# Moving half of a normalisation from VectorE to GpSimd at the head of its step, in the first pass of a two-pass expert FFN

## The chip, the core and the metric

The kernel runs on one core of one Trainium2 chip. The metric is the device time of one execution in microseconds (us), as a median of several runs.

## The reference

The input is 16384 tokens of 128 floats (256 x 64 positions). A first layer adds a gated pair-mixing block to it. The second layer, which the change concerns, is a mixture of eight experts, each token going to two of them:

```python
def _L0_ffn_ref(x, Wr, br, ln_g, ln_b, W1, b1, W2, b2):      # D = 128, E = 8 experts, H = 512
    probs = softmax(xt @ Wr + br)
    top_p, top_idx = top_k(probs, 2)
    weights = top_p / top_p.sum(axis=-1, keepdims=True)
    xn = (xt - mu) * rsqrt(var + 1e-5)
    xe = xn[None] * ln_g[:, None, :] + ln_b[:, None, :]
    h = gelu(einsum('end,edh->enh', xe, W1) + b1[:, None, :])
    y = einsum('enh,ehd->end', h, W2) + b2[:, None, :]
    out = (weights[:, :, None] * take_along_axis(y by token, top_idx)).sum(axis=1)
t = t + out
```

## The kernel before

Up to about 465 us of the profiled execution the kernel does the first layer, the choice of experts, and the scatter of each token's row (128 floats of data and a few of its own: scale `RS`, shift `SH`, weights, addresses) into a table in DRAM, sorted by expert. Then come two passes over tiles of 256 rows, 70 tiles each. A tile has two halves (`HALVES`, `b` = 0 and 1) of 128 rows. The first pass takes every token at its first expert, the second at its second. In the first pass a tile's rows are read from `row_dram`, normalised on the chip (the row's own `RS` and `SH`), and stored to `row2_dram` with the result added and with the normalised row beside it, so that the second pass has nothing to normalise.

Every engine runs its own queue, written out by `two_lists`: at step k it does each of its stages for the tile k minus that stage's lag, in the order of the list. Six slots (`RING`) hold the tiles; the body of the loop is six steps. In the first pass step k is:

- SyncE (`load_tile`): waits until both stores of tile k-6 have landed (`o_stored`, L339) and issues the load of a tile (L340). It runs ahead as far as the slots let it.
- VectorE: `norm(k)`, two operations, one for each half (L986); `xT_low(k-1)` (L991); `h_low(k-2)` for the first part (L996), `mix(k-3)` of half 0 (L1002), `h_low(k-2)` for the second part, `mix(k-3)` of half 1.
- TensorE: `xT(k-1)`, two transposes (L1158); `up(k-2)` in two parts (L1182 to L1184), with a reading of the experts' numbers between them in every sixth step (`next_experts`); `down(k-3)` (L1193 to L1204).
- ScalarE: `xT_high(k-1)` (L598), then `gelus(k-2)` in two parts (L605, L608).
- GpSimd: `store_tile(k-3)`, an indirect DMA for each half (L428), each after a wait for the `mix` of that half (`y_done`).

The names in the trace leave out numbers: `B` holds the tile's slots (`Rw`), `AB` the hidden values, `PPb` the split weights, `ps` PSUM.

Of the kernel before, what the change touches and what calls it, by code (L numbers as in the profile page):

```python
# [7 lines left out]
ALU = mybir.AluOpType  # L8
# [9 lines left out]
NE, D, H = 8, 128, 512  # L18
# [4 lines left out]
HALVES = 2  # L23
# [4 lines left out]
RING = 6  # L28
# [12 lines left out]
ROW = D + 8  # L41
ROW2 = ROW + D
R1, RS, SH, WLO, WHI, TOK, POS = range(D, D + 7)
# [19 lines left out]
def two_lists(eng, stages, depth, before=None, always=None):  # L63

    longest = max(lag for lag, _ in stages)
    for second, low, high in ((0, 0, CUT), (1, CUT, TILES)):

        def step(n, u):
            if before:
                before(n, u, low)  # L70
            for lag, stage in stages:
                if not isinstance(n, int) or low <= n - lag < high or stage is always and n + 1 < high + longest:
                    stage(n - lag, (u - lag) % RING, second)

        def single(n0, n1):
            for n in range(n0, n1):
                step(n, n % RING)

        first, last = -(-(low + longest + depth) // RING), high // RING
        single(low, first * RING)  # L80
        with eng.Fori(first, last) as t:
            for u in range(RING):
                step(t * RING + u, u)
        single(last * RING, high + longest)


def build(nc, x, pp, cp, z_mask, ln_w, ln_b, lnc_w, lnc_b, gate_w, gate_b, lin_w, lin_b, eg_w, eg_b,
          as_w, as_b, Wr, br, ffn_g, ffn_b, W1, b1, W2, b2, out, g_dram, row_dram, row2_dram):
    with ExitStack() as ctx:
# [3 lines left out]
        def sem(name):  # L93
            return ctx.enter_context(nc.semaphore(name))
# [88 lines left out]
        class Choice:  # L183
# [28 lines left out]
        Rw = Bf[:, 0:RING * HALVES * ROW2].rearrange("p (s b r) -> p s b r", s=RING, b=HALVES)  # L212
# [10 lines left out]
            "tail w_given rank_psum keep_set tail_done "  # L223
            "table Q_done tbl_psum cnt_done tbl_done pads_out pad_set "
            "gbM_step f_step ft_setup gb_kept am_done w1_sum w1_high w2_high b3f_dma "
            "store_next fill_done b23_zero xn_done xT_psum xT_hi xT_lo".split())}
        s = type("S", (), S)
        x_loaded = [sem(f"x_loaded{u}") for u in range(XRING)]
        pp_in = [[sem(f"pp_in{h}_{u}") for u in range(2)] for h in range(IC)]
# [8 lines left out]
        r_loaded = [sem(f"r_loaded{u}") for u in range(RING)]  # L238
# [10 lines left out]
        def _(sp):  # L249
# [64 lines left out]
            for table, blank, g0 in ((row_dram, pad, 0), (row2_dram, pad2, NE)):  # L314
                for q in range(0, NE, 4):
                    _, counts = nc.values_load_multi_w_load_instructions(nti[0:1, 1, g0 + q:g0 + q + 4], [mybir.EngineType.SP],
                                                                         min_val=0, max_val=N)
                    for k in range(4):
                        sp.dma_start(pair(table[bass.ds(counts[k] + (q + k) * CAP, TR), :]), blank).then_inc(s.pads_out, 16)
# [6 lines left out]
            for b, (_, j0, j1) in enumerate(BATCHES):  # L326
                sp.wait_ge(scattered[b], 16 * (j1 - j0))
# [17 lines left out]
        def _(pool):  # L345
# [84 lines left out]
                                            Rw[:, u, b, 0:D] if second else Rw[:, u, b, :], None,  # L430
                                            bounds_check=last_token if second else last_row, oob_is_err=False).then_inc(o_stored[u], 16)

            two_lists(pool, [(3, store_tile)], 1)
            for u in range(RING):
                pool.wait_ge(o_stored[u], 16 * HALVES * len(range(u, TILES, RING)))

# [1 line left out]
        def _(act):  # L438
# [65 lines left out]
            def weights(b):  # L504

                _, j0, j1 = BATCHES[b]
                act.wait_ge(s.tail, TAIL * b + 15)
                for at, scale in ((WLO, 1.0), (WHI, -1.0)):
                    a = act.activation(rows[:, j0:j1, at:at + 1].rearrange("p j o -> p (j o)"), choices[j1 - j0].m12[:, DL, :],
                                       ACT.Sigmoid, scale=scale)  # L510
                a.then_inc(s.w_given, 1)
# [101 lines left out]
        def _(dve):  # L613
# [339 lines left out]
            for e in range(NE):  # L953
                i = dve.scalar_tensor_tensor(W2h[:, e, 1, :, :], W2s[:, e, :, :], SCALE, W2h[:, e, 0, :, :], ALU.mult, ALU.subtract)
# [20 lines left out]
            for v, table in enumerate((first_row, experts[:, EFRONT:EFRONT + TILES])):  # L975
                i = dve.tensor_copy(table.rearrange("p (l t) -> p l t", l=LISTS),
                                    ps[6 + v][0:1, 0:LISTS * P].rearrange("p (l t) -> p l t", l=LISTS)[:, :, 0:CUT])
            i.then_inc(s.tbl_done, 1)

            def norm(n, u, second):  # L980

                if second:
                    return
                dve.wait_ge(r_loaded[u], (n // RING) * 16 + 16)
                for b in range(HALVES):
                    i = dve.tensor_scalar(Rw[:, u, b, ROW:ROW2], Rw[:, u, b, 0:D], Rw[:, u, b, RS:RS + 1], Rw[:, u, b, SH:SH + 1], ALU.mult, ALU.add)  # L986
                i.then_inc(s.xn_done, 1)

            def xT_low(n, u, second):
                dve.wait_ge(s.xT_hi, n + 1)  # L990
# [7 lines left out]
            def mix(n, u, second, b):  # L998
# [4 lines left out]
                                         ALU.mult, ALU.add).then_inc(y_done[b], 1)  # L1003

            two_lists(dve, [(0, norm), (1, xT_low), (2, lambda n, u, second: h_low(n, u, 0)), (3, lambda n, u, second: mix(n, u, second, 0)),
                            (2, lambda n, u, second: h_low(n, u, 1)), (3, lambda n, u, second: mix(n, u, second, 1))], 2)

        @block.tensor
        def _(pe):
# [54 lines left out]
            for h in range(IC):  # L1064
# [7 lines left out]
                for m in range(BANKS):  # L1072
# [7 lines left out]
                    for a in range(2):  # L1080
# [6 lines left out]
                        if m == 0 and a == 0:  # L1087
                            pe.wait_ge(s.abT_copied, h * 8 + 8)
                            pe.wait_ge(s.cp_done, 2)
                        i = pe.matmul(o.rearrange("p (x j) -> p x j", x=4)[:, 0::3, :], ABT[:, c // 2, :],  # L1090
                                      CPz[:, c:c + 2, :], start=False, stop=(a == 1))
# [53 lines left out]
            for k in range(2 * NQ):  # L1145
                i = pe.matmul(ps[6 + k // NQ][0:1, k % NQ * P:(k % NQ + 1) * P], Q[:, k:k + 1], ident[:, :], start=True, stop=True)
# [5 lines left out]
            def xT(n, u, second):  # L1152
                if second:
                    pe.wait_ge(r_loaded[u], (n // RING) * 16 + 16)
                else:
                    pe.wait_ge(s.xn_done, n + 1)
                for b in range(HALVES):
                    i = pe.transpose(ps[u % 2][:, b * P:(b + 1) * P], Rw[:, u, b, ROW:ROW2], ident[:, :])  # L1158
                i.then_inc(s.xT_psum, 1)
# [48 lines left out]
            def next_experts(n, u, second):  # L1208
                if u == RING - 1:
                    load_experts(n + 1)  # L1210

            two_lists(pe, [(1, xT), (2, lambda n, u, second: up(n, u, 0)), (0, next_experts), (2, lambda n, u, second: up(n, u, 1)),
                           (3, lambda n, u, second: down(n, u))], 2, before=begin, always=next_experts)

# [22 lines left out]
```

## Time and profile before

| | |
|---|---|
| three timed runs | 972.84, 979.42, 980.21 us (median 979.42) |
| the profiled execution | 973.23 us, its span 971.3 us |
| busy in the span | PE 737.7, VectorE 613.6, ScalarE 583.6, GpSimd 490.6 us |
| mean granted TensorE clock | 0.912 |

The span runs from the first to the last instruction; some 1.9 us of the profiled execution lie outside it. All times in the trace count from the span's start. The first pass fills the stretch from about 465 to 722 us, the second from there to the end. A busy share says what an engine did over the stretch, not whether others waited for it.

### The profile page before, as it was taken

What the parts mean: (1) busy time and instruction counts of PE and PEld (TensorE: products, weight loads), DVE (VectorE), ACT (ScalarE), POOL (GpSimd) and SP (SyncE); (2) the same over time, 40 slices, a digit from 0 to 9 for tenths busy, and PEclk for the clock granted to TensorE, in tenths of its full rate; (3) what the DMA queues carried; (4) which work ended last, traced back from release to release, by engine and by line L of the source; (5) the groups of instructions that cost most, each with busy time, mean ns of one, the idle gap of its engine ahead of it and who ended that gap; (6) DMA issues with size and microseconds to landing.
All of it is one profiled execution on the core that took longest, in us unless ns stands there. A gap on an engine that the chain in (4) does not pass through costs nothing. (4 is left out here: it accounts for less than half of the span.)

```text
span 971.3 us, 24094 instructions
## 1 busy us (share of the span) xinstructions
PE 737.7 (76%) x7308; PEld 644.9 (66%) x7309; DVE 613.6 (63%) x1866; ACT 583.6 (60%) x1162; POOL 490.6 (51%) x539
## 2 busy tenths in 40 slices
PE   1877899467696475622699999899859999999995
PEld 1655689255596365511588877778748888889884
DVE  6556510647843579876478777778746666667663
ACT  2667643579443366232477777767637777777773
POOL 4556500000177713777255555655644566666664
PEclk9989999679799588766799999999989999999998
DMA  7978510758113573415233333333323334434341
GB/s 217 236 226 260 153 55 10 228 147 261 58 57 120 181 231 108 163 55 200 70 114 114 113 119 113 117 106 114 111 65 110 116 113 120 125 115 127 117 130 30
DMA packets 127286, 126.86 MB, mean 131 GB/s; under 512 B 22472, under 2 KB 95455, under 8 KB 127107
## 3 DMA queue, kind: packets, MB, share of 16 engines
q1 hardware_dynamic: 92914, 82.73, 29.1%
q0 software_dynamic: 15296, 34.64, 10.1%
q10 hardware_dynamic: 19024, 8.86, 3.3%
q8 instruction: 26, 0.43, 0.2%
q14 instruction: 26, 0.21, 0.1%
HBM read 79.48 MB, written 49.09 MB: 132 GB/s over the span
## 5 line engine op out<-in xcount | busy, mean ns | idle before, releaser
L996 DVE TENSOR_TENSOR AB<-AB 128x512 f16<-128x512 f32 x280 | 192.2, 686 | 48.0 <-ACT AB L608 47.7
L399 POOL DMA_INDIRECT row_dram<-rows,idx x128 | 128.5, 1004 | 164.5 <-DVE rows L791 126.5
L605 ACT ACTIVATE AB<-ps 128x512 f16<-128x512 f32 x280 | 168.2, 601 | 56.2 <-PE ps L1184 55.9
L428 POOL DMA_INDIRECT row_dram<-B x140 | 143.4, 1025 | 115.4 <-DVE B L1002 79.3
L428 POOL DMA_INDIRECT out<-B x140 | 148.8, 1063 | 92.8 <-DVE B L1002 47.3
L1201 PE MATMUL ps<-PPb,AB 128*128 x1120 | 185.5, 219 | 0.0
L1202 PE MATMUL ps<-PPb,AB 128*128 x1120 | 185.4, 219 | 0.0
L1182 PE MATMUL ps<-B,PPb 128*128 128x256 f16 x560 | 154.7, 276 | 20.4 <-issue 10.2
L608 ACT ACTIVATE AB<-ps 128x512 f32<-128x512 f32 x280 | 168.9, 603 | 0.0
L1183 PE MATMUL ps<-B,PPb 128*128 128x256 f16 x560 | 154.2, 275 | 0.0
L1204 PE MATMUL ps<-PPb,AB 128*128 x1120 | 154.2, 219 | 0.0
L1184 PE MATMUL ps<-B,PPb 128*128 128x256 f16 x560 | 154.1, 275 | 0.0
L1002 DVE SCALAR_TENSOR_TENSOR B<-ps,B 128x128 f32<-128x128 f32 x280 | 97.2, 348 | 43.3 <-PE ps L1204 42.2
L598 ACT ACTIVATE B<-ps 128x256 f16<-128x256 f32 x140 | 53.7, 384 | 108.2 <-PE ps L1158 108.0
L1202 PEld LDWEIGHTS ps<-PPb,AB 128*128 128x128 f16 x1120 | 109.6, 98 | 0.0
L1201 PEld LDWEIGHTS ps<-PPb,AB 128*128 128x128 f16 x1120 | 108.6, 98 | 0.5
L1158 PE MATMUL ps<-ident,B 128*128 128x128 f32 x280 | 58.2, 290 | 46.4 <-DVE B L986 32.4
L1204 PEld LDWEIGHTS ps<-PPb,AB 128*128 128x128 f16 x1120 | 86.0, 98 | 0.0
L986 DVE TENSOR_SCALAR B<-B 128x128 f32<-128x128 f32 x140 | 44.0, 368 | 57.9 <-DMA B<-row_dram 57.2
L1182 PEld LDWEIGHTS ps<-B,PPb 128*128 x560 | 55.1, 98 | 36.3 <-issue 29.8
L1085 PE MATMUL ps<-AB,PPb 128*128 128x128 f32 x512 | 67.8, 276 | 1.2 <-DVE AB L698 1.2
L1045 PE MATMUL ps<-Wz,work 128*128 128x256 f32 x256 | 66.7, 408 | 0.7 <-ACT work L475 0.7
(214 smaller groups left out, 1350.2 us busy)
## 6 DMA issues: line engine op xcount, KB each, us to landing
B<-row_dram SPq DMA_DIRECT2D x70, 264.0 KB
B<-row_dram SPq DMA_DIRECT2D x70, 136.0 KB
rows<-in_x SPq DMA_DIRECT2D x32, 256.0 KB, 5.0
rows<-in_L_conv_protein_pair SPq DMA_DIRECT2D x16, 512.0 KB, 4.6
g_dram<-work ACTq DMA_DIRECT2D x32, 256.0 KB, 2.8
work<-g_dram SPq DMA_DIRECT2D x32, 256.0 KB, 3.9
ABT<-in_x SPq DMA_DIRECT2D x32, 256.0 KB, 4.2
ABT<-in_L_conv_protein_pair SPq DMA_DIRECT2D x16, 512.0 KB, 4.1
```

What stands on the lines that cost most here:

```text
L399: pool.indirect_dma_start(row_dram, bass.IndirectOffsetOnAxis(ap=idx[:, j:j + 1], axis=0), rows[:, j, :], None).then_inc(scattered[b], 16)
L428: pool.indirect_dma_start(out_rows if second else row2_dram, bass.IndirectOffsetOnAxis(ap=Rw[:, u, b, at:at + 1].bitcast(u32), axis=0), Rw ...
L605: act.activation(Hp[:, hs, 0, :], ps[HB[hs]][:, :], ACT.Gelu, scale=1.0 / SCALE)
L608: act.activation(Hf[:, q, :], ps[HB[hs]][:, :], ACT.Gelu, scale=1.0 / SCALE).then_inc(h_full[q], 1)
L996: dve.tensor_tensor(Hp[:, hs, 1, :], Hf[:, q, :], Hp[:, hs, 0, :], ALU.subtract).then_inc(h_parts[q], 1)
L1002: dve.scalar_tensor_tensor(Rw[:, u, b, 0:D], ps[4 + b][:, 0:D], Rw[:, u, b, w:w + 1], Rw[:, u, b, 0:D], ALU.mult, ALU.add).then_inc(y_done ...
L1182: pe.matmul(o, w(0), xTp[:, u % 2, 0, :], start=True, stop=False)
L1183: pe.matmul(o, w(0), xTp[:, u % 2, 1, :], start=False, stop=False)
L1184: i = pe.matmul(o, w(1), xTp[:, u % 2, 0, :], start=False, stop=True)
L1201: pe.matmul(ps[4 + b][:, 0:D], hk(0, b), w(0), start=False, stop=False)
L1202: pe.matmul(ps[4 + b][:, 0:D], hk(1, b), w(0), start=False, stop=False)
L1204: i = pe.matmul(ps[4 + b][:, 0:D], hk(0, b), w(1), start=False, stop=(k == HC - 1))
```

## The change

In the first pass `norm` on VectorE keeps half 0 only. GpSimd gets a new first stage of lag 0, `norm_second(k)`, which normalises half 1 of tile k, ahead of the stores of tile k-3 in its queue. TensorE's `xT` waits for both. In the second pass the new stage returns at once, as `norm` does.

```diff
@@ gpsimd
-            two_lists(pool, [(3, store_tile)], 1)
+            def norm_second(n, u, second):
+                if second:
+                    return
+                pool.wait_ge(r_loaded[u], (n // RING) * 16 + 16)
+                pool.sem_inc(s.store_next, 1)
+                pool.tensor_scalar(Rw[:, u, 1, ROW:ROW2], Rw[:, u, 1, 0:D], Rw[:, u, 1, RS:RS + 1], Rw[:, u, 1, SH:SH + 1],
+                                   ALU.mult, ALU.add).then_inc(s.xn_done2, 1)
+
+            two_lists(pool, [(0, norm_second), (3, store_tile)], 1)
@@ vector
                 dve.wait_ge(r_loaded[u], (n // RING) * 16 + 16)
-                for b in range(HALVES):
-                    i = dve.tensor_scalar(Rw[:, u, b, ROW:ROW2], Rw[:, u, b, 0:D], Rw[:, u, b, RS:RS + 1], Rw[:, u, b, SH:SH + 1], ALU.mult, ALU.add)
-                i.then_inc(s.xn_done, 1)
+                dve.tensor_scalar(Rw[:, u, 0, ROW:ROW2], Rw[:, u, 0, 0:D], Rw[:, u, 0, RS:RS + 1], Rw[:, u, 0, SH:SH + 1],
+                                  ALU.mult, ALU.add).then_inc(s.xn_done, 1)
@@ tensor
                     pe.wait_ge(s.xn_done, n + 1)
+                    pe.wait_ge(s.xn_done2, n + 1)
```

## Rows read from the trace of the kernel before

**Rows 1.** The busy time of each engine in one stretch (from the windows view).

```profile
core 0: us, PE busy (x) PEld busy (x) DVE busy (x) ACT busy (x) POOL busy (x), PEclk, DMA share, GB/s
600.00:620.00 20.00, 18.03 (x229) 15.98 (x227) 14.39 (x38) 14.06 (x29) 11.84 (x12) 1.00 0.37 116
```

**Rows 2.** Waits, 500 to 700 us: us in total, times, longest.

```profile
DVE B L986 <- DMA B<-row_dram: 35.5, 33, 3.0
...
PEld ps L1182 <- issue: 15.3, 24, 2.0
```

**Rows 3.** Waits of the queue of SyncE, 500 to 700 us.

```profile
SPq L339 <- DMA row_dram<-B: 103.7, 54, 4.2
```

**Rows 4.** Line L986: ns min/median/max, first and last start.

```profile
L986 DVE TENSOR_SCALAR B<-B x140: 331/346/609, 468.3 to 708.2; 128x128 f32<-128x128 f32 x140
```

**Rows 5.** Timeline of VectorE: start, us, operation, idle before and releaser.

```profile
573.14 0.59 DVE L986 TENSOR_SCALAR B<-B 128x128 f32<-128x128 f32 x2
...
575.00 0.35 DVE L1002 SCALAR_TENSOR_TENSOR B<-ps,B 128x128 f32<-128x128 f32 x1 [0.24 <-PE ps L1204]
...
577.81 0.68 DVE L986 TENSOR_SCALAR B<-B 128x128 f32<-128x128 f32 x2 [1.60 <-DMA B<-row_dram]
...
579.26 0.34 DVE L1002 SCALAR_TENSOR_TENSOR B<-ps,B 128x128 f32<-128x128 f32 x1
...
587.69 0.60 DVE L986 TENSOR_SCALAR B<-B 128x128 f32<-128x128 f32 x2 [1.08 <-DMA B<-row_dram]
```

**Rows 6.** Timeline of GpSimd, the same steps.

```profile
574.48 1.14 POOL L428 DMA_INDIRECT row_dram<-B  x1 [0.30 <-issue]
576.17 0.98 POOL L428 DMA_INDIRECT row_dram<-B  x1 [0.55 <-issue]
577.45 0.98 POOL L428 DMA_INDIRECT row_dram<-B  x1 [0.30 <-issue]
580.43 0.98 POOL L428 DMA_INDIRECT row_dram<-B  x1 [1.99 <-DVE B L1002]
581.72 0.98 POOL L428 DMA_INDIRECT row_dram<-B  x1 [0.30 <-issue]
```

**Rows 7.** Timeline of the queue of SyncE, one load.

```profile
584.99 0.54 SPq L340 DMA_DIRECT2D B<-row_dram  x1
```

**Rows 8.** Timeline of TensorE, the transposes of four steps.

```profile
568.83 0.43 PE L1158 MATMUL ps<-ident,B 128*128 128x128 f32 x2
...
571.86 0.39 PE L1158 MATMUL ps<-ident,B 128*128 128x128 f32 x2
...
574.85 0.39 PE L1158 MATMUL ps<-ident,B 128*128 128x128 f32 x2
...
578.54 0.44 PE L1158 MATMUL ps<-ident,B 128*128 128x128 f32 x2 [0.54 <-DVE B L986]
```

**Rows 9.** Timeline of weight loads, the first of `up`'s second part, some rounds.

```profile
503.47 0.10 PEld L1182 LDWEIGHTS ps<-B,PPb 128*128 x1 [0.76 <-issue]
...
525.43 0.10 PEld L1182 LDWEIGHTS ps<-B,PPb 128*128 x1 [1.61 <-issue]
...
609.37 0.10 PEld L1182 LDWEIGHTS ps<-B,PPb 128*128 x1 [2.00 <-issue]
...
713.54 0.10 PEld L1182 LDWEIGHTS ps<-B,PPb 128*128 x1 [0.89 <-issue]
```

**Rows 10.** Line L378, the first layer's normalisation on GpSimd.

```profile
L378 POOL TENSOR_SCALAR work<-rows x96: 441/445/552, 18.7 to 121.1; 128x128 f32<-128x128 f32 x96
```

**Rows 11.** Timeline of GpSimd: an indirect DMA and what follows it.

```profile
439.23 0.96 POOL L399 DMA_INDIRECT row_dram<-rows,idx  x1 [0.30 <-issue]
440.19 0.34 POOL L412 MEMSET work<- 128x272 f32 x1
```

**Rows 12.** Both engines at once (timelines), and line L996.

```profile
504.61 0.98 POOL L428 DMA_INDIRECT row_dram<-B  x1 [0.30 <-issue]
```

```profile
504.80 0.85 DVE L986 TENSOR_SCALAR B<-B 128x128 f32<-128x128 f32 x2 [1.49 <-DMA B<-row_dram]
```

```profile
L996 DVE TENSOR_TENSOR AB<-AB x280: 674/683/762, 473.8 to 957.7; 128x512 f16<-128x512 f32 x140
```

More of the change, by code:

```diff
@@ L225, in build @@
             "gbM_step f_step ft_setup gb_kept am_done w1_sum w1_high w2_high b3f_dma "
-            "store_next fill_done b23_zero xn_done xT_psum xT_hi xT_lo".split())}
+            "store_next fill_done b23_zero xn_done xn_done2 xT_psum xT_hi xT_lo".split())}
         s = type("S", (), S)
```

## The prediction

> **What bounds the kernel now.** I read the busy shares of a stretch of the first pass first. TensorE is busy 18.03 of 20 us, VectorE 14.39 and GpSimd 11.84 [rows 1]: at the mean step neither VectorE nor GpSimd is full, so a shift of work between them pays only where it shortens a chain. The step's mean comes from the first and last `norm`: (708.2 - 468.3) / 69 = 3.477 us [rows 4].
>
> The waits come next. VectorE's `norm` waited 33 times, 35.5 us in all, for the load of its tile [rows 2], and the load itself waited: SyncE stood 103.7 us, 54 times, at the stores of the tile that held the slot before [rows 3]. So the first pass runs in a ring through memory. Follow it in the timelines: `norm` starts at 577.81; `mix` of half 0 runs from 579.26 to 579.60; its store starts at 580.43 and the second store ends at 582.70; the load that needs the slot is issued at 584.99; the `norm` of that tile, three steps later, starts at 587.69, released by the DMA [rows 5 to 7]. That is 1.79 + 0.83 + 2.27 + 2.29 + 2.70 = 9.88 us for three steps; the mean of three steps is 10.43.
>
> The second chain to be read is the one through TensorE, which today has room. Its transposes at 571.86 open a step of TensorE, and the `mix` that ends that step starts at 575.00, released by TensorE; the stores follow at 576.17 and 577.45 and end at 578.43 [rows 5, 6, 8]. From transposes to end of stores: 6.57 us, made of 3.14 (TensorE's step), 0.35 (`mix`), 0.82 (to the start of the store) and 2.26 (two stores). One step earlier it is 575.62 - 568.83 = 6.79 [rows 6, 8]. TensorE's own step is 574.85 - 571.86 = 2.99 us.
>
> Third, TensorE has a stall of its own once in a round of six steps, ahead of the second part of `up`, where the experts' numbers are read: 0.76, then 1.61, and so on in turn, once 2.00, in a step whose transposes had begun late [rows 9]. Ten rounds lie between 503.47 and 713.54: 21.0 us each.
>
> **The change, part by part.**
>
> *VectorE loses one operation.* The pair takes 0.59 or 0.60 us and a single one 0.346 [rows 4, 5], so what goes is 0.25 us a step, 17.5 us of busy time over 70 steps. Of this only what stands in a binding chain counts. In the memory ring `norm` stands once per three steps, so the most that can come back is 0.25 x 70 / 3 = 5.8 us.
>
> *GpSimd gains one operation.* Its length is that of the same operation of the same shape in the first layer, 0.445 us [rows 10]. The nearest row for its start behind an indirect DMA is a memset that starts at 440.19, just as the DMA ends (439.23 + 0.96): no gap. Between two indirect DMAs there are 0.30 us [rows 11]. So the gap is 0 to 0.30; I take 0.05, since the 0.30 goes with the set-up of a DMA. GpSimd then needs 0.445 + 2.27 + 0.55 (the gap ahead of a tile's first store [rows 6]) + 0.05 = 3.3 us a step, against 3.48: GpSimd alone does not become the bound.
>
> *TensorE gains a wait, and here is the price.* The operation stands behind both stores of tile k-4 in GpSimd's queue, though its tile may have landed long before. Put it into today's rhythm. For the `norm` at 577.81 the stores end at 578.43, so half 1 is ready at 578.43 + 0.445 = 578.88, and with 0.05 us to the next engine (today's `norm` ends at 578.49 and the transposes start at 578.54) the transposes could start at 578.93, not 578.54 [rows 5, 6, 8]. For the `norm` at 573.14 the stores end at 575.62 and the transposes could start at 576.12, not 574.85 [rows 5, 6, 8]. So it is late by 0.4 and 1.3 us, and it is late in nearly every step. Behind the waiting transposes all of TensorE's step is queued: `up` of tile k-2 and `down` of tile k-3. On `down` waits `mix`, on `mix` the store, and behind the store stands the next normalisation but one. That closes a new ring of two steps: `norm_second(k-1)`, transposes of k-1, `down(k-3)`, `mix(k-3)`, `store_tile(k-3)`, `norm_second(k+1)`.
>
> Its length, low: 0.445 + 0.05 + 6.57 + 0 = 7.07 us; high: 0.445 + 0.05 + 6.79 + 0.30 = 7.59; taken, with the mean of the two samples: 0.445 + 0.05 + 6.68 + 0.05 = 7.23, or 3.61 a step. The stall for the experts falls on the same one of the two interleaved rings each time, since six is even, so it adds to every third turn of that ring, and the other can't run ahead of it. It is 1.2 (mean of 0.8 and 1.6) to 2.0; I take 1.6, because TensorE will now stand at its transposes in each step, as it had before the 2.00. A round of six steps is then 3 x 7.23 + 1.6 = 23.3 us against 21.0; low 3 x 7.07 + 1.2 = 22.4, high 3 x 7.59 + 2.0 = 24.8. The ring acts from about the fifth tile on, 65 steps or 10.8 rounds: (23.3 - 21.0) x 10.8 = +25 us, low +15, high +41.
>
> *Where the memory ring's waits go.* The load leaves the slot's stores behind by 2.29 + 2.70 = 5.0 us, the new `norm_second` comes some 7 us (two steps) after those stores: the tile has landed by then, and VectorE's 35.5 us of waiting for loads should almost vanish. The gain of 0.25 us on VectorE goes with them: it ends up as idle time. What is late next is TensorE, at its transposes.
>
> *The two engines side by side.* While GpSimd prepared a store at 504.61, VectorE's pair of normalisations took 0.85 us instead of 0.60 [rows 5, 12]: the two do get in each other's way, by some 0.25 us. The same could strike the new operation, against `h_low`, which comes twice in VectorE's step. No row shows a GpSimd operation that reads its memory beside `h_low`; the bounds are 0 and one whole `h_low`, 0.68 us [rows 12]. I take 0, since in the new ring the operation starts as `mix` starts, after the first `h_low` and before the second.
>
> The Trainium skill speaks against the change here ("SBUF — State Buffer", Who interferes with whom): VectorE and GpSimd share one pair of ports under an exclusive lock, and a VectorE instruction with two inputs in SBUF, as `h_low` has, excludes a GpSimd instruction that reads SBUF for its whole length. The stretched pair agrees with it for the other kind of VectorE instruction. By the rule taken at its worst the new operation would wait behind an `h_low` in every turn of the ring, which is the second rival below.
>
> Removed and added waits of VectorE and the increments of semaphores I put at nothing; the second pass keeps its instructions but for GpSimd's empty stage, and moves as a whole.
>
> **The sum.** 973.23 (this execution) + 25 = 998. This execution is one of the low ones: the timed runs go from 972.84 to 980.21 with a median of 979.42, and on the median the sum is 1004. I forecast the middle, 1001.
>
> **The rivals.**
>
> 1. *The stall is swallowed.* If TensorE's sequencer reads the experts' numbers while it stands at the transposes, the round is 3 x 7.07 to 3 x 7.3, 21.2 to 21.9 us, +2 to +10 us: 975 to 990. For it: the stall halves in every second round. Against it: it was longest where TensorE had just stood at the transposes.
> 2. *The port decides.* Each turn of the new ring gets 0.68 us more behind an `h_low`: 3 x 0.68 x 10.8 = +22 on top of 25: 1020 to 1027. For it: the 0.85 us pair. Against it: the place of the operation in the ring.
> 3. *Not slower: the memory ring stays the bound, and VectorE's part of it is shorter.* -5.8 us at most: 967 to 974. It decides if the operation ends before TensorE is at its transposes, that is, if GpSimd's stores end at least 0.5 us (0.445 + 0.05) before them. Today they end 0.1 us before at 578.54 and 0.8 us after at 574.85, so it would take another rhythm. For it: GpSimd is only 59% busy [rows 1].
> 4. *The change does not matter*, because the operations run as said but TensorE's step stretches into slack that I haven't seen: within 5 us of before, 973 to 985.
>
> **How the numbers follow.** Forecast 0.60 (988 to 1020, from 973.2 + 15 to 979.4 + 41), the swallowed stall 0.17, the port 0.10, the shorter memory ring 0.07, no matter 0.06. Leaving out the last two and the lower part of the first rival gives 984; the top reaches into the port's case, 1023. One per cent, 9.8 us, is about what a measurement of this kernel can tell from no change: under 969.6 is the lower half of rival 3, 0.04; within it are the rest of 3, rival 4 and half of rival 1, 0.17; slower 0.79.
>
> **What would show it.** In the profile after: TensorE's transposes (L1158's successor) wait for GpSimd in nearly every step, some 0.5 us each, and that group leads the idle time of TensorE in the first pass; the waits for loads fall from 35.5 us to a few; SyncE waits longer for stores only because steps are longer; first to last `norm` is about 240 + 25 = 265 us; the GpSimd operation starts as the second store ends and takes 0.43 to 0.45 us; `h_low` keeps its 683 ns. The prediction is wrong if the transposes go on without a wait, if GpSimd's queue has the operation ahead of the stores' wait in time as well as in order, or if the second pass changes its length.

## The result and the profile after

The changed kernel takes 1028.28 us (median of four, 1024.18 to 1031.86) against 979.82 us (median of four): a ratio of 1.0507, 95% interval 1.0435 to 1.0578. That is 48 us slower, where 1001 us (984 to 1023) was forecast. The profiled execution took 1031.23 us, its span 1029.5.

Three views of the profile after say where the time went. First the windows view, the waits and SyncE's waits (500 to 700 us), for the stretches of [rows 1 to 3]. L1167 is now the transposes, L439 GpSimd's normalisation, L994 VectorE's, L1004 `h_low`, L1010 `mix`.

```profile
600.00:620.00 20.00, 15.97 (x203) 14.23 (x201) 12.98 (x30) 12.22 (x26) 14.12 (x15) 1.00 0.29 93
```

```profile
PEld ps L1167 <- issue: 39.4, 39, 1.6
PE ps L1167 <- POOL B L439: 33.7, 38, 1.5
...
PEld ps L1191 <- issue: 11.9, 8, 1.9
...
DVE B L994 <- DMA B<-row_dram: 6.8, 17, 1.7
```

```profile
SPq L339 <- DMA row_dram<-B: 121.0, 46, 5.5
```

VectorE's wait for loads, 35.5 us before, is down to 6.8, and TensorE stands at its transposes for GpSimd instead, 33.7 us in 38 waits, about 0.9 us each, in some 47 steps. SyncE stands longer at the stores, 121.0 us against 103.7, but it runs ahead, and no engine waits much for its loads. The memory ring has let go and the ring through the stores has taken over.

The lines of the two normalisations, to be set against [rows 4] and [rows 10] (min/median/max in ns, first and last start):

```profile
L439 POOL TENSOR_SCALAR B<-B x70: 447/662/1027, 471.2 to 764.7; 128x128 f32<-128x128 f32 x70
```

```profile
L994 DVE TENSOR_SCALAR B<-B x70: 328/345/391, 471.0 to 763.1; 128x128 f32<-128x128 f32 x70
```

From the first to the last `norm` there are 292.1 us, 4.23 a step, against 239.9 and 3.48: the first pass holds 52 us of the difference of the spans, 58.2; the rest lies ahead of the first `norm` (2.7) and behind the last (3.3). And GpSimd's operation takes 0.66 us at the median, where 0.445 was forecast.

One turn of each of the two interleaved rings, in the timelines of GpSimd, VectorE and TensorE:

```profile
597.39 0.65 POOL L439 TENSOR_SCALAR B<-B 128x128 f32<-128x128 f32 x1
...
600.54 0.88 POOL L439 TENSOR_SCALAR B<-B 128x128 f32<-128x128 f32 x1
602.52 1.02 POOL L428 DMA_INDIRECT row_dram<-B  x1 [1.10 <-DVE B L1010]
603.84 1.50 POOL L428 DMA_INDIRECT row_dram<-B  x1 [0.30 <-issue]
605.35 0.66 POOL L439 TENSOR_SCALAR B<-B 128x128 f32<-128x128 f32 x1
606.18 1.02 POOL L428 DMA_INDIRECT row_dram<-B  x1 [0.17 <-DVE B L1010]
607.51 0.99 POOL L428 DMA_INDIRECT row_dram<-B  x1 [0.30 <-issue]
608.52 0.87 POOL L439 TENSOR_SCALAR B<-B 128x128 f32<-128x128 f32 x1
```

```profile
600.41 0.69 DVE L1004 TENSOR_TENSOR AB<-AB 128x512 f16<-128x512 f32 x1 [0.94 <-ACT AB L617]
601.35 0.35 DVE L1010 SCALAR_TENSOR_TENSOR B<-ps,B 128x128 f32<-128x128 f32 x1 [0.24 <-PE ps L1213]
...
603.79 0.69 DVE L1004 TENSOR_TENSOR AB<-AB 128x512 f16<-128x512 f32 x1 [0.59 <-ACT AB L617]
604.72 0.35 DVE L1010 SCALAR_TENSOR_TENSOR B<-ps,B 128x128 f32<-128x128 f32 x1 [0.24 <-PE ps L1213]
604.99 0.71 DVE L1004 TENSOR_TENSOR AB<-AB 128x512 f16<-128x512 f32 x1
```

```profile
601.57 0.41 PE L1167 MATMUL ps<-ident,B 128*128 128x128 f32 x2 [0.20 <-POOL B L439]
...
606.16 0.41 PE L1167 MATMUL ps<-ident,B 128*128 128x128 f32 x2 [1.42 <-POOL B L439]
```

Normalisation 600.54 to 601.42, transposes 601.57, `mix` 604.72 to 605.07, store 606.18, end of the second store 608.50, next normalisation but one 608.52: 0.88 + 0.15 + 3.15 + 0.35 + 1.11 + 2.32 + 0.02 = 7.98 us for two steps. It is the forecast ring link by link. Two links are clearly longer than forecast: the normalisation, and the way from `mix` to the store, 1.11 instead of 0.82. The other ring, from 597.39 to 605.35, is 0.65 + 3.31 + 0.35 + 0.82 + 2.82 + 0.01 = 7.96 us, and there the pair of stores is the long link, 2.82 us instead of 2.27.

Where do these come from? The normalisation at 600.54 starts when the `h_low` of 600.41 has 0.56 us left, and takes 0.41 us more than the 0.47 that it takes when nothing is beside it. The one at 605.35 starts when the `h_low` of 604.99 has 0.35 left, and takes 0.19 more. The store at 603.84 starts when the `h_low` of 603.79 has 0.64 left, and takes 1.50 instead of 0.98. And the store at 606.18 comes 0.29 later than its `mix` asks for, because the other ring's normalisation, itself put off by the long store, has just been done ahead of it. So each ring gets 0.70 us a turn more: 0.41 + 0.29 in the one, 0.18 + 0.51 in the other.

The third view is the place where the experts' numbers are read. Windows, and TensorE's timeline, once in twelve steps:

```profile
536.00:539.00 3.00, 1.42 (x11) 0.96 (x12) 1.46 (x3) 1.47 (x3) 2.68 (x3) 0.88 0.21 51
539.00:542.50 3.50, 3.50 (x34) 3.23 (x33) 0.19 (x1) 1.09 (x2) 0.16 (x1) 0.62 0.23 76
540.00:541.00 1.00, 1.00 (x12) 1.00 (x10) 0.00 (x0) 0.92 (x2) 0.00 (x0) 0.50 0.03 8
542.50:546.00 3.50, 2.82 (x39) 2.51 (x36) 3.00 (x8) 2.45 (x5) 2.21 (x2) 1.00 0.25 78
```

```profile
535.94 0.41 PE L1167 MATMUL ps<-ident,B 128*128 128x128 f32 x2 [1.42 <-POOL B L439]
...
538.58 0.39 PE L1191 MATMUL ps<-B,PPb 128*128 128x256 f16 x1 [1.58 <-issue]
...
542.17 0.39 PE L1167 MATMUL ps<-ident,B 128*128 128x128 f32 x2
```

TensorE had waited 1.42 us at the transposes and then 1.58 us for the reading, and then its granted clock fell: 0.50, the lower of its two levels (1.2 and 2.4 GHz), from 540 to 541, and 0.62 in the mean from 539.0 to 542.5. The step from 535.94 took 6.23 us. From 480 to 720 us the mean granted clock is 0.96 in the changed kernel and 1.00 in the kernel before. From 542.17 to the same place twelve steps later (593.54) there are 51.4 us: 6 turns of 7.97, 0.8 for the milder reading and 2.9 for this one.

### The profile page after: what moved, and what is told of

Same layout as the page of the kernel before. It is cut to its first block and busy times, and to the rows that moved or that the text cites. A ratio compares the mean times of both kernels' runs of the same rounds, so it can differ in the third digit from the quotient of the medians.

```text
span 1029.5 us, 24264 instructions
## 1 busy us (share of the span) xinstructions
PE 747.6 (73%) x7308; PEld 657.2 (64%) x7309; DVE 605.9 (59%) x1796; ACT 584.2 (57%) x1162; POOL 551.8 (54%) x609
## 5 line engine op out<-in xcount | busy, mean ns | idle before, releaser
L1004 DVE TENSOR_TENSOR AB<-AB 128x512 f16<-128x512 f32 x280 | 194.0, 693 | 97.0 <-ACT AB L617 96.1
L428 POOL DMA_INDIRECT row_dram<-B x140 | 151.9, 1085 | 101.0 <-DVE B L1010 78.0
L1210 PE MATMUL ps<-PPb,AB 128*128 x1120 | 189.1, 222 | 0.0
L1211 PE MATMUL ps<-PPb,AB 128*128 x1120 | 189.1, 222 | 0.0
L1191 PE MATMUL ps<-B,PPb 128*128 128x256 f16 x560 | 157.0, 280 | 23.5 <-issue 13.0
L1192 PE MATMUL ps<-B,PPb 128*128 128x256 f16 x560 | 156.9, 280 | 0.0
L1193 PE MATMUL ps<-B,PPb 128*128 128x256 f16 x560 | 156.7, 280 | 0.0
L1213 PE MATMUL ps<-PPb,AB 128*128 x1120 | 156.5, 222 | 0.0
L1010 DVE SCALAR_TENSOR_TENSOR B<-ps,B 128x128 f32<-128x128 f32 x280 | 96.8, 346 | 72.7 <-PE ps L1213 72.5
L1167 PE MATMUL ps<-ident,B 128*128 128x128 f32 x280 | 58.8, 293 | 91.4 <-POOL B L439 78.0
L1211 PEld LDWEIGHTS ps<-PPb,AB 128*128 128x128 f16 x1120 | 111.7, 100 | 0.0
L1210 PEld LDWEIGHTS ps<-PPb,AB 128*128 128x128 f16 x1120 | 111.6, 100 | 0.0
L1167 PEld LDWEIGHTS ps<-ident,B 128*128 128x128 f32 x280 | 29.4, 146 | 104.8 <-issue 61.1
L1213 PEld LDWEIGHTS ps<-PPb,AB 128*128 128x128 f16 x1120 | 88.0, 100 | 0.0
L1191 PEld LDWEIGHTS ps<-B,PPb 128*128 x560 | 56.0, 100 | 35.8 <-issue 29.8
L999 DVE TENSOR_TENSOR B<-ps,B 128x256 f16<-128x256 f32 x140 | 58.4, 417 | 29.3 <-ACT B L607 29.1
```

The source lines that it names most:

```text
L428: pool.indirect_dma_start(out_rows if second else row2_dram, bass.IndirectOffsetOnAxis(ap=Rw[:, u, b, at:at + 1].bitcast(u32), axis=0), Rw ...
L1004: dve.tensor_tensor(Hp[:, hs, 1, :], Hf[:, q, :], Hp[:, hs, 0, :], ALU.subtract).then_inc(h_parts[q], 1)
L1010: dve.scalar_tensor_tensor(Rw[:, u, b, 0:D], ps[4 + b][:, 0:D], Rw[:, u, b, w:w + 1], Rw[:, u, b, 0:D], ALU.mult, ALU.add).then_inc(y_done ...
L1191: pe.matmul(o, w(0), xTp[:, u % 2, 0, :], start=True, stop=False)
L1192: pe.matmul(o, w(0), xTp[:, u % 2, 1, :], start=False, stop=False)
L1193: i = pe.matmul(o, w(1), xTp[:, u % 2, 0, :], start=False, stop=True)
```

## The experiments

The stretch is first to last `norm` in the profiled execution; the column "before" is the kernel before, measured beside each. The experiments set two theories against each other: A, the ring through the order of GpSimd's queue; B, the mere work of two engines on one memory. In the two kernels "`h_low` from PSUM" and in the one with both edits, `h_low` subtracts another number than the one it should: they leave out the low part of the hidden values, so their result is not the layer's, and they serve for the time alone.

| kernel | median us | before | ratio (95%) | stretch us |
|---|---|---|---|---|
| before | | | | 239.9 |
| changed | 1028.28 | 979.82 | 1.0507 (1.0435 to 1.0578) | 292.1 |
| order only | 1006.25 | 980.53 | 1.0292 (1.0230 to 1.0354) | 268.0 |
| work only | 986.34 | 980.53 | 1.0066 (1.0036 to 1.0095) | 247.4 |
| changed, `h_low` from PSUM | 1012.58 | 980.53 | 1.0338 (1.0275 to 1.0401) | 273.3 |
| before, `h_low` from PSUM | 978.48 | 980.53 | 0.9978 (0.9942 to 1.0014) | 240.4 |
| stores one step further back | 1033.35 | 979.90 | 1.0519 (1.0448 to 1.0589) | 295.7 |
| behind the stores | 1390.48 (one run) | 979.90 | | 641.4 |
| changed, numbers read first | 1009.32 | 979.90 | 1.0310 (1.0246 to 1.0373) | 266.6 |
| ScalarE does half 1 | 993.53 | 979.90 | 1.0148 (1.0077 to 1.0219) | 254.7 |
| changed, both edits | 995.69 | 982.62 | 1.0140 (1.0073 to 1.0207) | 257.0 |
| before, numbers read first | 980.44 | 982.62 | 0.9985 (0.9949 to 1.0022) | 241.2 |

**The order without the work.**

```diff
@@ gpsimd, norm_second
-                pool.tensor_scalar(Rw[:, u, 1, ROW:ROW2], ...).then_inc(s.xn_done2, 1)
+                pool.memset(spare[:, u, 0:1], 0.0).then_inc(s.xn_done2, 1)
@@ vector, norm: both halves again
```

> The order without the work: GpSimd keeps the new stage at the head of its step, but writes one column of a spare area there instead of normalising; VectorE does both halves again; TensorE's transposes still wait for both engines. Theory A (a ring of two steps through the order of GpSimd's queue): a turn is 0.1 + 0.15 + 3.15 + 0.35 + 0.82 + 2.3 = 6.9 us, six steps 20.7 us and 1.2 to 2.0 us for the reading of the experts' numbers, 21.9 to 22.7 against 21.0 in the kernel before: 990 to 998 us, and the transposes wait for GpSimd. Theory B (not the order, but the work of two engines on one memory port makes the kernel slower): as the kernel before, 973 to 983 us.

1006.25 us, 26 us over before: the order costs half of the whole, without any work moved. TensorE waits for GpSimd (waits view, 500 to 700 us):

```profile
PE ps L1168 <- POOL AB L440: 25.7, 26, 1.2
```

The turn is longer than the 6.9 expected, 7.1 to 7.3 us, and this is why (GpSimd's timeline; from the memset at 593.90 the next but one is at 601.09, 7.19 us later):

```profile
593.90 0.14 POOL L440 MEMSET AB<- 128x1 f32 x1
594.28 0.98 POOL L429 DMA_INDIRECT row_dram<-B  x1 [0.24 <-issue]
595.57 0.98 POOL L429 DMA_INDIRECT row_dram<-B  x1 [0.30 <-issue]
596.52 0.14 POOL L440 MEMSET AB<- 128x1 f32 x1
598.51 0.98 POOL L429 DMA_INDIRECT row_dram<-B  x1 [1.85 <-DVE B L1011]
599.80 1.31 POOL L429 DMA_INDIRECT row_dram<-B  x1 [0.30 <-issue]
```

Every other second store takes 1.2 to 1.4 us here too. The one at 599.80 starts inside an `h_low`, and in the kernel before the store of 1.14 us at 574.48 [rows 6] does as well (VectorE's timelines, this kernel and the kernel before):

```profile
599.57 0.68 DVE L1005 TENSOR_TENSOR AB<-AB 128x512 f16<-128x512 f32 x1
```

```profile
574.06 0.69 DVE L996 TENSOR_TENSOR AB<-AB 128x512 f16<-128x512 f32 x1
```

So this kernel is not free of collisions: about 0.25 us of a turn, some 8 us of the 26 by an estimate from the turns (33 turns), are stores stretched by `h_low`. The expectation had the shape right and missed 8 us at its upper end.

**The work without the order.**

```diff
@@ gpsimd, norm_second
-                pool.tensor_scalar(Rw[:, u, 1, ROW:ROW2], ...).then_inc(s.xn_done2, 1)
+                pool.tensor_scalar(spare[:, u, :], ...).then_inc(s.xn_done2, 1)
@@ vector: norm does both halves again; mix of half 1 waits for xn_done2
@@ tensor, xT
-                    pe.wait_ge(s.xn_done2, n + 1)
```

> The work without the order: VectorE does both halves as before and TensorE waits for VectorE alone; GpSimd normalises half 1 once more at the head of its step, into a spare area, and only the mix of the same tile, three steps later, waits for it. Theory A: no ring, GpSimd's stores are at most 0.3 to 0.5 us later in some steps, 975 to 990 us. Theory B: the contention is all there, so is the time: about 1028 us.

986.34 us, 6 us over before, within theory A's numbers. Theory B by itself is out. Yet most of the collisions are there (line L440, its normalisation): at the median it takes 0.657 us, as in the changed kernel, and in the mean 0.666 against 0.725.

```profile
L440 POOL TENSOR_SCALAR AB<-B x70: 447/657/1033, 470.0 to 718.4; 128x128 f32<-128x128 f32 x70
```

So a collision costs little when nobody waits for it. What it costs inside the ring is the next experiment.

**The collisions taken away.** The second input of `h_low` comes from PSUM, the sum ahead of the gelu in place of the rounded half.

```diff
@@ vector, h_low
-                dve.tensor_tensor(Hp[:, hs, 1, :], Hf[:, q, :], Hp[:, hs, 0, :], ALU.subtract)...
+                dve.tensor_tensor(Hp[:, hs, 1, :], Hf[:, q, :], ps[HB[hs]][:, :], ALU.subtract)...
```

> The changed kernel, with the second input of h_low read from PSUM (the sum before the gelu) instead of the rounded half in SBUF, so that no VectorE instruction of a step has two inputs in SBUF; the low parts of the hidden values are no longer what they should be. If the collisions with h_low are what lengthens the turn of the ring from 7.23 to 7.97 us: GpSimd's normalisation takes 0.45 to 0.48 us in each step instead of 0.66 and 0.88, the second store 0.98 instead of 1.49, six steps 3 x 7.3 + 1.5 = 23.4 us instead of 25.7, about 1003 us. If the shared port has nothing to do with it: 1025 to 1032 us.

1012.58 us, 16 us less than the changed kernel. `h_low` itself takes what it took, 679 ns, but the normalisation is at 0.47 us every time and no indirect store is over 1.03 us (both lines, then GpSimd's timeline):

```profile
L439 POOL TENSOR_SCALAR B<-B x70: 448/472/493, 470.1 to 743.9; 128x128 f32<-128x128 f32 x70
```

```profile
L428 POOL DMA_INDIRECT row_dram<-B x140: 982/991/1032, 480.3 to 756.5; - x140
```

```profile
545.73 0.47 POOL L439 TENSOR_SCALAR B<-B 128x128 f32<-128x128 f32 x1
546.56 1.02 POOL L428 DMA_INDIRECT row_dram<-B  x1 [0.37 <-issue]
547.89 0.99 POOL L428 DMA_INDIRECT row_dram<-B  x1 [0.30 <-issue]
548.89 0.48 POOL L439 TENSOR_SCALAR B<-B 128x128 f32<-128x128 f32 x1
```

The turn is 7.27 us in nearly all cases, against 7.97, and 7.23 was forecast without collisions. The median is 10 us over the expected 1003. About 3 of them are the expectation's own arithmetic: its 2.4 us a round come to 1006. Most of the others are the reading, which takes 1.0 + 3.2 us in twelve steps here, where 3.0 were put in.

This kernel also shows what the clock costs by itself. The readings at 532.68 and 579.02 hold TensorE up alike (1.89 and 1.85 us ahead of the weights), but only the second is followed by a fall of the clock:

```profile
531.00:534.00 3.00, 1.39 (x19) 1.25 (x19) 0.99 (x2) 1.53 (x3) 1.56 (x3) 1.00 0.43 134
579.00:582.00 3.00, 2.97 (x23) 2.65 (x24) 0.30 (x1) 1.08 (x2) 0.43 (x1) 0.53 0.33 92
```

The turns over the first take 9.06 and 9.23 us, over the second 10.66 and 10.47: the fall costs 1.4 us a time.

**The control.** The same edit of `h_low` in the kernel before.

> The kernel before with the same edit of h_low, to see what that edit does by itself: 968 to 983 us by both theories; if collisions of stores and h_low matter before too, the lower end.

978.48 us, no difference that can be told, though the longest store of the first pass falls from 1.45 to 1.03 us. That the collisions sit in a slack part of the ring there is argued, not shown.

**One step more of lead.** The fix that comes to mind first: let GpSimd normalise a step earlier, so that TensorE never waits.

```diff
-            two_lists(pool, [(0, norm_second), (3, store_tile)], 1)
+            two_lists(pool, [(0, norm_second), (4, store_tile)], 1)
```

> The changed kernel with GpSimd's normalisation one step further ahead of its stores: the stores of tile k-4 instead of k-3 behind the normalisation of tile k. Theory A: the ring through TensorE now takes three steps for the same 8 us and stops to bind, but the normalisation of tile k waits for its load, and the stores of k-4 behind it release the load of k+2: a ring of two steps through memory, 0.45 to 0.88 + 0.17 + 2.3 + 2.3 to 2.9 + 2.7 = 7.9 to 8.9 us, 4.0 to 4.45 us a step, so 1010 to 1046 us, with GpSimd waiting for loads instead of TensorE for GpSimd. If only the ring through TensorE counted, the lead would cure it: 970 to 985 us.

1033.35 us: no better, for another reason, as expected. The wait for the load of tile k now holds back the stores of k-4, on which the load of k+2 hangs. GpSimd's waits (500 to 700 us) and timeline:

```profile
POOL B L439 <- DMA B<-row_dram: 47.8, 46, 2.1
```

```profile
553.97 0.49 POOL L439 TENSOR_SCALAR B<-B 128x128 f32<-128x128 f32 x1 [0.80 <-DMA B<-row_dram]
...
558.22 0.49 POOL L439 TENSOR_SCALAR B<-B 128x128 f32<-128x128 f32 x1 [0.95 <-DMA B<-row_dram]
```

4.25 us for this step and 4.28 in the mean of the pass, inside the 4.0 to 4.45 worked out.

**Behind the stores.**

```diff
-            two_lists(pool, [(0, norm_second), (3, store_tile)], 1)
+            two_lists(pool, [(3, store_tile), (0, norm_second)], 1)
```

> The changed kernel with the normalisation of tile k behind the stores of tile k-3 instead of ahead. Theory A: the transposes of tile k then hang on the stores of k-3, and the next normalisation on the stores that follow those transposes' own step: the same 7.2 to 8 us, but in a ring of one step. First to last normalisation 69 x 7.2 to 8.0 = 497 to 552 us against 292: 1230 to 1290 us. Theory B: the same work and the same contention, about 1028 us.

1390.48 us, in a single run. With the same instructions in another order the ring closes in one step and the first pass takes 641 us. It is theory A's sign and scale, but over its upper end by 100 us. The windows view and GpSimd's timeline tell why:

```profile
600.00:640.00 40.00, 23.08 (x161) 18.83 (x160) 10.33 (x24) 10.04 (x21) 9.91 (x12) 0.67 0.13 41
```

```profile
606.71 0.47 POOL L439 TENSOR_SCALAR B<-B 128x128 f32<-128x128 f32 x1
...
617.12 0.47 POOL L439 TENSOR_SCALAR B<-B 128x128 f32<-128x128 f32 x1
```

TensorE idles between its short steps, its granted clock is at 0.67 in the mean, and its link of the ring grows from 3.15 to between 4.5 and 6.5 us, so nearly all turns are 8.6 to 10.6 us. I had costed it at full clock.

**The reading ahead of the transposes.**

```diff
-            two_lists(pe, [(1, xT), (2, ... up 0), (0, next_experts), (2, ... up 1),
+            two_lists(pe, [(0, next_experts), (1, xT), (2, ... up 0), (2, ... up 1),
```

> The changed kernel with TensorE's reading of the experts' numbers at the head of its step, ahead of the transposes, instead of between the two parts of up. If the stall of this reading lies in the ring, it now hides behind the wait for GpSimd, which is 0.2 to 1.4 us a step, and the clock has no reason to fall: of 3.7 us lost in twelve steps (0.8, and 2.9 with the lower clock) up to all comes back, 20 us: 1008 to 1018 us. If the stall is somebody else's wait: 1028 us as before.

1009.32 us, 19 us less than the changed kernel. The reading hides behind the wait for GpSimd, and `up`'s second part no longer idles ahead of its weights. The clock's falls go with it: the mean granted clock from 480 to 720 us is 0.99 against 0.96. But the edit does more than it was meant to do: the two rings now stand otherwise to each other, and 24 of 62 turns take 7.26 to 7.79 us instead of 7.97, against 6 of 62 in the changed kernel. That is some 5 us of the 25.5 that the stretch gets shorter, by the sum of those turns (weight loads of L1191, 500 to 700 us, of the changed kernel and of this one):

```profile
L1191 PEld LDWEIGHTS ps<-B,PPb 128*128 x184 | 18.4, 100 | 13.9 <-issue 11.9
```

```profile
L1191 PEld LDWEIGHTS ps<-B,PPb 128*128 x206 | 20.1, 98 | 2.6
```

**ScalarE instead of GpSimd.**

```diff
@@ gpsimd: as in the kernel before
-            two_lists(pool, [(0, norm_second), (3, store_tile)], 1)
+            two_lists(pool, [(3, store_tile)], 1)
@@ scalar
+            def norm_second(n, u, second):          # ScalarE
+                act.wait_ge(r_loaded[u], (n // RING) * 16 + 16)
+                act.activation(Rw[:, u, 1, ROW:ROW2], Rw[:, u, 1, 0:D], ACT.Identity, bias=Rw[:, u, 1, SH:SH + 1],
+                               scale=Rw[:, u, 1, RS:RS + 1]).then_inc(s.xn_done2, 1)
-            two_lists(act, [(1, xT_high), ...
+            two_lists(act, [(0, norm_second), (1, xT_high), ...
```

> Half 1 normalised by ScalarE at the head of its step, GpSimd as in the kernel before. Theory A: no ring through the stores, so most of the 48 us come back; but ScalarE waits for the load ahead of its gelus, which puts up to 1.1 us into the memory ring of three steps: 970 to 1000 us. Theory B (two engines at one port): nothing left of the contention, 968 to 980 us.

993.53 us, 1.5% over before and 35 us under the changed kernel. ScalarE now waits for the loads (500 to 700 us) ahead of its gelus:

```profile
ACT B L614 <- DMA B<-row_dram: 55.7, 45, 3.7
```

It is in the range of theory A. That this wait is the price of the 14 us that remain is argued, not shown.

**Both edits at once**, `h_low` from PSUM and the reading first, in the changed kernel.

> The changed kernel with both edits: h_low's second input from PSUM, and the reading of the experts' numbers ahead of the transposes. If ring, collisions and the stall with its low clock are the whole account, only the bare ring is left, 7.27 us in two steps: 6 x 7.27 = 43.6 us in twelve steps against 42.0 in the kernel before, so 980 + 1.6 x 5.4 = 989 us, 984 to 994. If the two edits took the same time away twice, or something else lengthens the first pass: over 996 us.

995.69 us against 982.62 beside it, 13 us over before where 9 were expected, and 2 us above the range. The turn is 7.27 us in most cases; every twelve steps two turns still get some 0.7 us more where TensorE starts its transposes late, and four turns from 684 to 706 us take 9.3 to 10.0, which is 5 us of the pass. The same tiles (58 to 61) are late in the changed kernel's trace too, 8.8 to 10.5 us; what holds them up stays open. In the stretch the `h_low` edit takes 18.8 us away, the reading 25.5, both together 35.1, so 9 us of the two are the same. Some 5 of these are the collisions that the reading's edit had removed already; the rest is open. This kernel is as near as the experiments come to the bare ring: 13 us.

**Is there a gain for the kernel before?** The reading ahead of the transposes, in the kernel before, twelve runs:

> The kernel before with the reading of the experts' numbers ahead of the transposes. There TensorE does not stand at its transposes in most steps, so the reading has less to hide behind; in the first pass the memory ring binds and the stall of 1.2 us in six steps was partly slack: 970 to 980 us, a gain of under 1%. If the stall counts in full in both passes (1.2 us in 23 rounds), 953 us.

980.44 against 982.62 us, ratio 0.9985 (0.9949 to 1.0022): none that can be told. None of the kernels tried beats the kernel before.

## Why the prediction was wrong

*What bounds the kernel now* held. The memory ring was the bound, and its waits vanished as forecast (35.5 us to 6.8).

*The price of the new wait* held in its mechanism, link by link: a ring of two steps through both stores, TensorE's step and `mix`. The order without the work costs 26 us, the work without the order 6. The sign that was given in advance came true in kind, the transposes waiting for GpSimd, at about 0.9 us a time instead of 0.5.

*The gap behind a DMA*, taken as 0.05, is 0.02. The way from GpSimd to TensorE, taken as 0.05, is 0.15. These two are small and nearly cancel in a turn of 7.27 against 7.23 forecast.

*The two engines side by side* is the step that failed. I had the row that showed a collision [rows 12], had the rule of the Trainium skill, bounded the cost by 0 and 0.68 us a turn, and took 0, arguing that the operation starts as `mix` starts, after the first `h_low` and before the second. The turn measured 7.97 us, 0.70 more than without collisions (7.27). The operation at 605.35 starts 0.63 after the `mix` of 604.72, inside the second `h_low`; the one at 600.54 starts 0.81 before the `mix` of 601.35, inside the first. The argument had tacitly taken the steps to be evenly spaced, and the two interleaved rings are not (600.54, 605.35, 608.52). Nor were the stores counted, though [rows 6] held one of 1.14 us: the indirect DMA itself is stretched, up to 1.50 us, and it lies in the ring even where nothing is normalised. In twelve steps that is 6 x 0.74 = 4.4 us against the forecast turn, 24 us over 65 steps.

*The reading of the experts' numbers* was in the sum at 1.6 a round, 3.2 in twelve steps. It measured 0.8 + 2.9 = 3.7: another 3 us. A fall of TensorE's clock, 1.4 us a time where it could be told apart, was a term that the sum did not have; without it the two stalls come to some 2.3 us, less than was put in. With these, 25 + 24 + 3 = 52 us, the stretch's 52. That the sum closes so well is in part luck, since the late tiles 58 to 61 are not in it.

*The second rival*, the port, gave 1020 to 1027 with a chance of 0.10, and is what happened, a little more than it gave. Its price per turn, 0.68, was right to 0.02 by luck: no turn waits for a whole `h_low`; each ring has two shorter delays, and one of the two falls on its stores. The chance was too low, and my range did not reach its end. The Trainium skill ("SBUF — State Buffer", Who interferes with whom) says that a VectorE instruction with two SBUF inputs and a GpSimd instruction that reads SBUF exclude each other. This case's runs agree (0.66 and 0.88 us with such an `h_low`, 0.47 without), save that the time added is 0.15 us less than what the `h_low` had left.

*The first rival*, a swallowed stall, needed another order of TensorE's queue: it came true only when the reading was put ahead of the transposes. The third, not slower, did not show: GpSimd's stores ended too late in 38 of some 47 steps. The fourth, no matter, is out by 48 us.

## What to carry over

When a step is moved to another engine, write down what stands ahead of it in that engine's queue and follow the ring until it closes; divide its length by the number of steps that it spans. Half of this loss was there with no work moved at all, and one place further down the queue, in one run, cost another 360 us. A bound between 0 and one whole instruction is not settled by where the instruction would stand in an even rhythm: take the middle, or widen the range to the end. And an idle piece that was harmless becomes dear once the engine already waits elsewhere in the step.

## What the runs showed of the hardware

An indirect DMA that GpSimd prepares is stretched by `h_low` as well: at most 1.50 us in the kernels with two SBUF inputs, at most 1.03 in those without, 0.98 at rest. Of the stores of the first pass that start with over 0.3 us of an `h_low` left, 13 in the kernel before (0.42 left in the mean) take 0.30 us more than 0.98, 28 in the kernel with the order only (0.48) take 0.36 more, 25 in the changed kernel (0.56) take 0.44 more. With the second input from PSUM, 13 and 16 such stores (0.43) take nothing more. So the kernel before had it too. "SBUF — State Buffer", Who interferes with whom, in the Trainium skill infers that a `tensor_tensor` does not get in the way of the making of descriptors; these stores, which take their addresses from SBUF, differ, and the measurement decides. That the addresses are the reason is not shown.

`h_low` can be the one that is stretched, but only where GpSimd normalises. In the kernel with the work only, one takes 0.97 instead of 0.68 us; a store of 1.07 us runs beside it, and GpSimd's normalisation begins at 602.75, before its end (timelines of VectorE and GpSimd). In the kernel before and in the one with the order only, 80 and 74 `h_low` start beside a store, and none takes over 0.69.

```profile
602.12 0.97 DVE L1006 TENSOR_TENSOR AB<-AB 128x512 f16<-128x512 f32 x1
```

```profile
601.66 1.07 POOL L429 DMA_INDIRECT row_dram<-B  x1 [0.30 <-issue]
```

And TensorE's clock: in the changed kernel the engine had been busy for 1.42 of 3.0 us ahead of a stretch with a mean granted clock of 0.62, and the clock was back at 1.00 right after; in the kernel with the normalisation behind the stores TensorE was busy for 23.08 of 40 us at a mean clock of 0.67. How much longer the waits of a slow order make the work itself I had not expected.
